# Scaling of the second norm on ScalarE instead of VectorE, in an attention and mixture-of-experts kernel

## The chip, the cores and the metric

The kernel runs on one core of one Trainium2 chip. The time is the device time of one execution in microseconds. An execution is one launch; several runs were made, and their median is the kernel's time. TensorE (PE, with its weight loads PEld), VectorE (DVE), ScalarE (ACT), GpSimd (POOL) and SyncE (SP) each work through their own list of instructions in order and meet through semaphores.

## The reference

The inputs are 4 sequences of 512 tokens with 256 features and, for each, a context of 64 tokens.

```python
x = x + xattn(layernorm(x), ctx, ctx, Wq, bq, Wk, bk, Wv, bv, We, be)   # 16 heads of 16
x = x + ffn(layernorm(x), router_w, router_b, expert_up, expert_down)

def ffn(x):                                  # 8 experts, 1024 hidden, the best 2 per token
    probs = softmax(x @ router_w + router_b)
    top_w, top_idx = top_k(probs, 2)
    for e in range(8):
        h = gelu(x @ expert_up[e].T)
        output += comb[:, e:e+1] * (h @ expert_down[e].T)
```

The layer norm has no learned scale: `(x - mean) / sqrt(var + 1e-5)`. The change is in the second one, ahead of the router.

## The kernel before

The work has two stages. The first takes the four sequences (batches) in turn: norm, attention, residual, second norm, router, and the place of each token in its expert's list. The second walks over tiles of 128 rows gathered by expert. Each engine's program is written by hand, in the order in which it is to run, and a loop step `batch(i)` works on two or three batches at once: it ends batch i−1 (attention output, second norm, logits), begins batch i (queries, scores, exponentials) and, from i = 2 on, does the routing of batch i−2. There are three such steps (i = 1, 2, 3), called steps 1, 2 and 3 here, and then a tail that ends the last batch alone.

A batch is four tiles of 128 tokens (`LT` = 4). Around the second norm this happens:

- VectorE, `residual_norm2` (line 766): for each half (two tiles) it adds the attention's output to `xall` (771), takes statistics (776, 781) and writes `var2` (783). GpSimd makes `rstd2` from it by a power of −0.5 (`halves_rstd2`, 347, line 345). After both halves VectorE scales all four tiles into `xr` (789), by mean and rstd per row. Then come the routing's one-hots of batch i−2, `puts` (872, lines 877 and 879), eight pairs in a ring of four buffers, so the fifth pair waits until TensorE has used the first; and then `logits` (795), whose first instruction is `lg` (798).
- TensorE: `project_out`, `max_turn` (turned maxima, 1165), `scores_turned` of pairs 0 to 3 (1171; pair 3 waits for the first exponential, whose bank it takes), `x2_turn` (turns `xr` into features by tokens, 1240), `slots` (1282), `logits` (1249), `logits_turn` (1255), `slots` again. The next step begins with `values` (1195, 1196), which waits for `lg`.
- ScalarE: `max_turn` (copies the turned maxima, 494), `exps` 0 to 3 (503), `x2_turn` (copies the turned tiles to `x2T`, 525), `logit_copy` (530), `router_exp` (534).
- SyncE: `store` writes `xall` to `out` and `xr`, with the routing weights in its last 8 columns, to `rows` (315). The second stage gathers from `rows`. Before the weights of experts 2 to 7 overwrite `xall`, SyncE waits for the stores of `xall` (325).

The semaphore `v_xn2` counts the scaled tiles; only TensorE's `x2_turn` waits for it (1237).

Of the kernel before, what the change touches and what calls it, by code (L numbers as in the profile page):

```python
# [102 lines left out]
def build(nc, x, ctx_t, ctx_t2, wq, wk, wv, we, bqk, bv, be, router_w, router_b, up, down, const, out, rows):  # L103
    with ExitStack() as ctx:
# [6 lines left out]
        def sem(name):  # L111
            return ctx.enter_context(nc.semaphore(name))
# [4 lines left out]
        def c(name):  # L117
# [44 lines left out]
        mv2 = sb("mv2", [P, LT, 2])  # L162
        var2 = sb("var2", [P, LT])
        rstd2 = sb("rstd2", [P, LT])
        xr = sb("xr", [P, LT, XROW])
        x2T = sb("x2T", [P, LT, KD, P])
        lg, lgs, ex, pr = (sb(n, [P, LT, NE]) for n in ("lg", "lgs", "ex", "pr"))
# [75 lines left out]
            sem(n) for n in "v_wsplit v_k v_stat1 v_var1 v_xn v_xT v_q v_max".split())  # L243
        v_nmh, v_nml, v_rden, v_rdh, v_rdl, v_att, v_at, v_x1 = (
            sem(n) for n in "v_nmh v_nml v_rden v_rdh v_rdl v_att v_at v_x1".split())
        v_stat2, v_var2, v_xn2, v_lg, v_pr, v_top, v_mk, v_msum = (
            sem(n) for n in "v_stat2 v_var2 v_xn2 v_lg v_pr v_top v_mk v_msum".split())
        v_seen, v_comb, v_mbf, v_mtot, v_pos, v_key, v_hot, v_put = (
            sem(n) for n in "v_seen v_comb v_mbf v_mtot v_pos v_key v_hot v_put".split())
        v_pack, v_tab, v_slot, v_done, v_fxT, v_gate, v_fhT, v_y = (  # L250
# [17 lines left out]
        @block.sync  # L268
        def _(sp):
            x_t = x.rearrange("(t p) d -> p t d", p=P)  # L270
            sp.dma_start(xall[:, 0:LT, :], x_t[:, 0:LT, :]).then_inc(d_x0, 16)
            sp.dma_start(cst[:, 0:EARLY], const[:, 0:EARLY]).then_inc(d_const, 16)

            def rows_of(a):
                return a.rearrange("(k p) n -> p k n", p=P)

            def raw_w(n):
                return wraw[:, n, :].rearrange("p (k n) -> p k n", k=KD)


            sp.dma_start(raw_w(1), rows_of(wk)).then_inc(d_k, 16)
            sp.dma_start(ctxT[:, :, :], rows_of(ctx_t)).then_inc(d_k, 16)
            sp.dma_start(bias[:, :, :], bqk.rearrange("p (j k) -> p j k", k=KD)).then_inc(d_k, 16)
            sp.dma_start(raw_w(0), rows_of(wq)).then_inc(d_q, 16)
            sp.dma_start(xall[:, LT:NTOK, :], x_t[:, LT:NTOK, :]).then_inc(d_x, 16)
            sp.dma_start(raw_w(2), rows_of(wv)).then_inc(d_v, 16)
            sp.dma_start(ctxT2[:, :, :, :].rearrange("p k b s -> p k (b s)"), rows_of(ctx_t2)).then_inc(d_v, 16)
            sp.dma_start(raw_w(3), rows_of(we)).then_inc(d_we, 16)
            sp.dma_start(cst[:, EARLY:NCONST], const[:, EARLY:NCONST]).then_inc(d_sel, 16)
            sp.wait_ge(g_rw, 1)  # L290
            sp.dma_start(rw[:, :, 0:NE], rows_of(router_w)).then_inc(d_w, 16)
            sp.dma_start(bv_b[:, :], bv.rearrange("(a n) -> a n", a=1).broadcast_to([P, D])).then_inc(d_w, 16)
            sp.dma_start(be_b[:, :], be.rearrange("(a n) -> a n", a=1).broadcast_to([64, D])).then_inc(d_w, 16)
            sp.dma_start(rb[:, :], router_b.rearrange("(a n) -> a n", a=1).broadcast_to([P, NE])).then_inc(d_w, 16)

            sp.wait_ge(g_zero, 2)
            zeros = zero_r[:, :].bitcast(F32)
            zeros_d = zeros.rearrange("p (a n) -> p a n", a=1).broadcast_to([P, KD, P])
            sp.dma_start(rows[T:T + P, 0:D].rearrange("p (a n) -> p a n", a=KD), zeros_d).then_inc(d_zero, 16)
            sp.dma_start(rows[T:T + P, D:XROW], zeros[:, 0:NE]).then_inc(d_zero, 16)  # L300
            sp.dma_start(out[T:T + P, :].rearrange("p (a n) -> p a n", a=KD), zeros_d).then_inc(d_zero, 16)


            def load01(i):
                if not (isinstance(i, int) and i == 0):
                    sp.wait_ge(v_w01, 2 * i)
                sp.dma_start(raw01[:, 0, :], up[bass.ds(i, 1)].rearrange("a p n -> (a p) n")).then_inc(d_raw01, 16)
                sp.dma_start(raw01[:, 1, :], down[bass.ds(i, 1)].rearrange("a p n -> (a p) n")).then_inc(d_raw01, 16)

            def store(g):  # L310
                sp.wait_ge(v_x1, 2 * g + 2)
                sp.dma_start(out[bass.ds(g * L, L), :].rearrange("(t p) d -> p t d", p=P),
                             xall[:, bass.ds(g * LT, LT), :]).then_inc(d_x1, 16)
                sp.wait_ge(v_comb, g + 1)
                sp.dma_start(rows[bass.ds(g * L, L), :].rearrange("(t p) d -> p t d", p=P),
                             xr[:, :, :]).then_inc(d_rows, 16)

            load01(0)
            with sp.Fori(1, B) as i:
                load01(i)  # L320
                store(i - 1)
            store(B - 1)


            sp.wait_ge(d_x1, 16 * B)
            for e in range(2, NE):
                for q in range(8):
                    if e > 2 and q % 2 == 0:
                        sp.wait_ge(v_wlo, 8 + 4 * (e - 3) + q // 2 + 1)
                    src = (up if q < 4 else down)[2 * e + q // 2 % 2]  # L330
                    sp.dma_start(raw[:, q * 512:(q + 1) * 512], src[:, (q % 2) * 512:(q % 2 + 1) * 512])\
                        .then_inc(d_rawu if q < 4 else d_rawd, 16)
# [119 lines left out]
        def _(act):  # L452
# [64 lines left out]
            def att_high(b):  # L517
                for k in range(KD):
                    act.wait_ge(v_att, KD * b + k + 1)
                    a.activation(at_h[:, k, :], av[:, k, :], ACT.Identity).then_inc(a_at, 1)  # L520

            def x2_turn(b):
                for n in range(2):
                    act.wait_ge(p_x2T, 2 * b + n + 1)
                    a.activation(x2T[:, 2 * n:2 * n + 2, :, :].rearrange("p t k l -> p (t k l)"), bankA[:, n, :], ACT.Identity)\
                        .then_inc(a_x2T, 1)
# [38 lines left out]
            def batch(i):  # L565
                av_copy(i - 1, 0)
                x_high(i, 0)
                exps(i - 1, range(4, 8))
                x_high(i, 1)
                den_copy(i - 1)  # L570
                av_copy(i - 1, 1)
                q_high(i)
                rden_turn(i - 1)
                att_high(i - 1)
                high01(i)
                max_turn(i)
                exps(i, range(4))
                x2_turn(i - 1)
                logit_copy(i - 1)
                router_exp(i - 1)  # L580
# [6 lines left out]
            av_copy(B - 1, 1)  # L587
            rden_turn(B - 1)
            att_high(B - 1)
            x2_turn(B - 1)  # L590
            logit_copy(B - 1)
            router_exp(B - 1)
# [70 lines left out]
        def _(dve):  # L663
# [102 lines left out]
            def residual_norm2(b):  # L766

                for n in range(2):
                    dve.wait_ge(p_proj, 2 * b + n + 1)
                    xs = xall[:, bass.ds(b * LT + 2 * n, 2), :]  # L770
                    v.tensor_tensor(xs, bankB[n][:, :].rearrange("p (t d) -> p t d", t=2), xs, ALU.add)\
                        .then_inc(v_x1, 1)
                    dve.wait_ge(v_x1, 2 * b + n + 1)
                    settle(5)
                    for k in (2 * n, 2 * n + 1):
                        v.bn_stats(stat2[:, k, :], xall[:, bass.ds(b * LT + k, 1), :]
                                   .rearrange("p a d -> p (a d)")).then_inc(v_stat2, 1)
                    dve.wait_ge(v_stat2, 8 * b + 4 * n + 2)
                    settle(6)
                    for k in (2 * n, 2 * n + 1):  # L780
                        v.bn_aggr(mv2[:, k, :], stat2[:, k, :]).then_inc(v_stat2, 1)
                    dve.wait_ge(v_stat2, 8 * b + 4 * n + 4)
                    v.tensor_scalar(var2[:, 2 * n:2 * n + 2], mv2[:, 2 * n:2 * n + 2, 1], EPS, None, ALU.add)\  # L783
                        .then_inc(v_var2, 1)
                if not (isinstance(b, int) and b == 0):
                    dve.wait_ge(d_rows, 16 * b)
                for k in range(LT):
                    dve.wait_ge(g_rstd2, 2 * b + k // 2 + 1)
                    v.tensor_scalar(xr[:, k, 0:D], xall[:, bass.ds(b * LT + k, 1), :].rearrange("p a d -> p (a d)"),
                                    mv2[:, k, 0:1], rstd2[:, k:k + 1], ALU.subtract, ALU.mult).then_inc(v_xn2, 1)  # L790

            def bc3(ap, n):
                return ap.rearrange("p (q a) -> p q a", a=1).broadcast_to([P, ap.shape[1], n])
# [306 lines left out]
        def _(pe):  # L1100
# [133 lines left out]
            def x2_turn(b):  # L1234
                for n in range(2):
                    for t in range(2):
                        pe.wait_ge(v_xn2, LT * b + 2 * n + t + 1)
                        for k in range(KD):
                            o = (t * KD + k) * P
                            last = nc.tensor.transpose(bankA[:, n, o:o + P], xr[:, 2 * n + t, k * P:(k + 1) * P], ident)  # L1240
                    last.then_inc(p_x2T, 1)
# [223 lines left out]
```

## Time and profile before

| | |
|---|---|
| median of 3 runs | 467.22 us (465.77 to 470.2) |
| the profiled execution | 466.3 us, of it 464.5 us span |
| first stage | until about 192 us, the rest is the second stage |
| busy: PE, DVE, ACT, POOL | 85%, 53%, 42%, 36% of the span |
| mean granted TensorE clock | 0.934 of full |

The span runs from the first instruction to the last. A group's busy time says how long an engine worked, not that anything waited for it; the chain of waits says what ended last, and the order in time says what an engine did between. "Granted clock" is the share of TensorE's full clock that the throttle let through: 1.00 is 2.4 GHz, 0.50 is 1.2 GHz. The times at the start of a row are microseconds from the start of the span.

### The profile page before, as it was taken

The numbers are of one execution on the slowest core, as the hardware profiler recorded it, in microseconds if no ns is written. First come the engines' busy times: TensorE is split into PE (matmuls) and PEld (weight loads), VectorE is DVE, ScalarE is ACT, GpSimd is POOL, SyncE is SP. The second block draws the span as 40 slices with busy tenths as digits, with TensorE's granted clock in tenths as the row PEclk, the third lists the DMA queues.
The fourth block names the chain that finished last, engine by engine and source line by source line (L and its number), as shares of the span: only waits on it lengthen the run. The fifth ranks groups of instructions, "written<-read, shape, count | busy, mean of one in ns | idle before, by whom it ended". The sixth has DMA issues, their size and how long they took to land.

```text
span 464.5 us, 9448 instructions
## 1 busy us (share of the span) xinstructions
PE 396.3 (85%) x2154; PEld 315.9 (68%) x2155; DVE 244.7 (53%) x693; ACT 194.2 (42%) x356; POOL 166.0 (36%) x266
## 2 busy tenths in 40 slices
PE   3799897889988674499999899989898999999970
PEld 2575675666666452278888787878787888888860
DVE  3394768887789455723336437364554355333230
ACT  1265433333434312034437346556473464354430
POOL 2315022020301000224454554554546536545541
PEclk9799999998999955589999999999999999999995
DMA  8702010410401101711223627262736222222221
GB/s 277 279 2 90 1 47 0 139 45 1 137 0 54 39 0 48 244 29 24 49 34 93 168 34 215 46 204 48 211 81 173 42 36 46 34 38 42 46 34 11
DMA packets 24784, 36.49 MB, mean 79 GB/s; under 512 B 3136, under 2 KB 15872, under 8 KB 24768
## 3 DMA queue, kind: packets, MB, share of 16 engines
q1 hardware_dynamic: 17760, 26.44, 16.8%
q0 software_dynamic: 7008, 9.86, 13.4%
q8 instruction: 7, 0.11, 0.1%
q14 instruction: 9, 0.07, 0.0%
HBM read 27.04 MB, written 9.24 MB: 78 GB/s over the span
## 4 chain that ended last, share of the span: by engine, by line
PE 56%; issue 16%; DMA 7%; DVE 7%; POOL 5%; ACT 4%; POOLq 1%; ACTq 1%; SPq 0%; DVEq 0%
PE bankC L1385 10%; PE bankC L1106 7%; PE bankC L1108 7%; PE bankC L1107 7%; DMA xr<-rows,idx_g 5%; PE bankC L1386 5%; PE bankB L1363 5%; PE bankA L1355 2%; PE bankB L1106 2%; POOL idx_g L408 2%; PE bankA L1195 1%; PE bankM L1282 1%; POOL rstd L345 1%; PE bankB L1108 1%; PE bankB L1107 1%
## 5 line engine op out<-in xcount | busy, mean ns | idle before, releaser
L1385 PE MATMUL bankC<-dn_w,q_h 128*128 x288 | 104.7, 403 | 1.2 <-DVE q_l L1041 1.2
L1386 PE MATMUL bankC<-dn_w,q_l 128*128 x288 | 80.6, 280 | 0.0
L425 POOL DMA_INDIRECT out<-x2T,idx_s x36 | 58.0, 1612 | 21.3 <-issue 21.3
L1385 PEld LDWEIGHTS bankC<-dn_w,q_h 128*128 128x128 f32 x288 | 54.1, 188 | 12.4 <-issue 1.4
L1106 PE MATMUL bankC<-up_w,xnT_h 128*128 (+1 forms) x144 | 61.0, 424 | 0.9 <-DVE xnT_l L1035 0.9
L1048 DVE SCALAR_TENSOR_TENSOR x2T<-bankC,gate,x2T 128x256 f32<-128x256 f32 x36 | 17.4, 483 | 81.7 <-ACT x2T L614 63.2
L1108 PE MATMUL bankC<-up_w,xnT_l 128*128 (+1 forms) x144 | 57.9, 402 | 0.0
L1107 PE MATMUL bankC<-up_w,xnT_h 128*128 (+1 forms) x144 | 57.5, 399 | 0.0
L1386 PEld LDWEIGHTS bankC<-dn_w,q_l 128*128 128x128 f32 x288 | 54.2, 188 | 0.0
L609 ACT ACTIVATE raw<-bankC 128x512 f32<-128x512 f32 x72 | 43.1, 599 | 24.6 <-PE bankC L1108 24.6
L414 POOL DMA_INDIRECT xr<-rows,idx_g x38 | 42.6, 1120 | 22.3 <-issue 21.7
L1041 DVE TENSOR_TENSOR q_l<-bankB,q_h 128x512 fp32r<-128x512 f32 x72 | 46.1, 681 | 0.8 <-ACT q_h L605 0.7
L345 POOL TENSOR_TENSOR rstd<-var,cst 128x2 f32<-128x2 f32 (+2 forms) x10 | 9.4, 938 | 94.5 <-DVE var L783 87.3
L614 ACT ACTIVATE x2T<-bankC,gate 128x256 f32<-128x256 f32 x36 | 17.0, 472 | 60.6 <-PE bankC L1386 58.6
L389 POOL TENSOR_TENSOR prime<-prime 1x1 f32<-1x1 f32 x74 | 13.7, 185 | 76.4 <-DVE x2T L1048 64.6
L605 ACT ACTIVATE q_h<-bankB 128x512 fp32r<-128x512 f32 x72 | 38.9, 595 | 0.3 <-PE bankB L1363 0.3
L1363 PE MATMUL bankB<-cst,raw 128*128 128x128 f32 x288 | 37.5, 273 | 0.5 <-ACT raw L609 0.5
L600 ACT ACTIVATE xnT_h<-bankA 128x256 fp32r<-128x256 f32 x37 | 14.3, 388 | 53.1 <-PE bankA L1355 51.9
L1363 PEld LDWEIGHTS bankB<-cst,raw 128*128 128x128 f32 x288 | 32.8, 141 | 2.2 <-ACT raw L609 0.8
L408 POOL COPY idx_g<-slot 128x1 int32 (+1 forms) x38 | 28.7, 754 | 15.6 <-DVE slot L972 14.9
L1035 DVE TENSOR_TENSOR xnT_l<-bankA,xnT_h 128x256 fp32r<-128x256 f32 x37 | 15.6, 423 | 32.5 <-ACT xnT_h L600 32.5
L1108 PEld LDWEIGHTS bankC<-up_w,xnT_l 128*128 128x128 f32 x144 | 27.6, 192 | 6.7
(215 smaller groups left out, 726.9 us busy)
## 6 DMA issues: line engine op xcount, KB each, us to landing
xall<-up SPq DMA_DIRECT2D x24, 256.0 KB
xall<-down SPq DMA_DIRECT2D x24, 256.0 KB
rows<-xr SPq DMA_DIRECT2D x4, 528.0 KB, 3.3
raw<-up SPq DMA_DIRECT2D x4, 512.0 KB, 4.5
raw<-down SPq DMA_DIRECT2D x4, 512.0 KB, 5.4
out<-xall SPq DMA_DIRECT2D x4, 512.0 KB, 2.8
xall<-x SPq DMA_DIRECT2D x1, 1536.0 KB, 8.5
cst<-const SPq DMA_DIRECT2D x1, 640.0 KB, 8.4
```

The source lines that it names most:

```text
L408: g.tensor_copy(idx_g[:, ring:ring + 1], slot[:, bass.ds(col, 1)]).then_inc(g_gi, 1)
L414: g.indirect_dma_start(xr[:, ring, :], None, rows, bass.IndirectOffsetOnAxis(idx_g[:, ring:ring + 1], 0), bounds_check=T + P - 1).then_inc ...
L425: g.indirect_dma_start(out, bass.IndirectOffsetOnAxis(idx_s[:, 0:1], 0), y, None, bounds_check=T + P - 1, compute_op=ALU.add).then_inc(d_a ...
L605: a.activation(hT_h[:, n * 512:(n + 1) * 512], bankB[n][:, :], ACT.Identity).then_inc(a_fhT, 1)
L609: a.activation(hbuf[:, n * 512:(n + 1) * 512], bankC[:, n, :], ACT.Gelu).then_inc(a_gelu, 1)
L1041: v.tensor_tensor(hT_l[:, o], bankB[n][:, :], hT_h[:, o].bitcast(F32), ALU.subtract)\
L1106: mm(out_, left_h, right_h, start=first, stop=False)
L1107: mm(out_, left_h, right_l, start=False, stop=False)
L1108: return mm(out_, left_l, right_h, start=False, stop=last)
L1363: last = nc.tensor.transpose(bankB[n][:, m * P:(m + 1) * P], hbuf[:, o:o + P], ident)
L1385: mm(bankC[:, 2, :], hT_h[:, o], wd, start=(m == 0), stop=False)
L1386: last = mm(bankC[:, 2, 0:D], hT_l[:, o], wd[:, 0:D], start=False, stop=(m == KF - 1))
```

## The change

VectorE no longer scales the tiles. For each half it computes `nmr2` = −mean · rstd, two columns. ScalarE does the scaling as `Identity(scale · x + bias)` with `scale` = `rstd2` and `bias` = `nmr2`, a column each, for the two tiles of a half. In a loop step the first half's two activations stand between ScalarE's `max_turn` and the first exponential, the second half's between the second and the third exponential; in the tail both stand ahead of `x2_turn`. The semaphore that counts the scaled tiles is now ScalarE's. SyncE waits for the last scaling before it loads over `xall`, since ScalarE now reads `xall` last.

```diff
+        nmr2 = sb("nmr2", [P, LT])
...
             sp.wait_ge(d_x1, 16 * B)
+            sp.wait_ge(a_xn2, LT * B)
...
+            def norm2(b, n):
+                act.wait_ge(v_nmr, 2 * b + n + 1)
+                for k in (2 * n, 2 * n + 1):
+                    a.activation(xr[:, k, 0:D], xall[:, bass.ds(b * LT + k, 1), :].rearrange("p a d -> p (a d)"),
+                                 ACT.Identity, bias=nmr2[:, k:k + 1], scale=rstd2[:, k:k + 1]).then_inc(a_xn2, 1)
...
                 max_turn(i)
-                exps(i, range(4))
+                norm2(i - 1, 0)
+                exps(i, range(2))
+                norm2(i - 1, 1)
+                exps(i, range(2, 4))
                 x2_turn(i - 1)
...
             att_high(B - 1)
+            norm2(B - 1, 0)
+            norm2(B - 1, 1)
             x2_turn(B - 1)
...
-                for k in range(LT):
-                    dve.wait_ge(g_rstd2, 2 * b + k // 2 + 1)
-                    v.tensor_scalar(xr[:, k, 0:D], xall[:, bass.ds(b * LT + k, 1), :].rearrange("p a d -> p (a d)"),
-                                    mv2[:, k, 0:1], rstd2[:, k:k + 1], ALU.subtract, ALU.mult).then_inc(v_xn2, 1)
+                for n in range(2):
+                    dve.wait_ge(g_rstd2, 2 * b + n + 1)
+                    v.scalar_tensor_tensor(out=nmr2[:, 2 * n:2 * n + 2], in0=mv2[:, 2 * n:2 * n + 2, 0], scalar=-1.0,
+                                           in1=rstd2[:, 2 * n:2 * n + 2], op0=ALU.mult, op1=ALU.mult).then_inc(v_nmr, 1)
...
-                        pe.wait_ge(v_xn2, LT * b + 2 * n + t + 1)
+                        pe.wait_ge(a_xn2, LT * b + 2 * n + t + 1)
```

## Rows read from the trace of the kernel before

**Rows 1.** The page's first part: busy us, share of the span, instructions.

```profile
PE 396.3 (85%) x2154; PEld 315.9 (68%) x2155; DVE 244.7 (53%) x693; ACT 194.2 (42%) x356; POOL 166.0 (36%) x266
```

**Rows 2.** The chain of waits, end of step 1: start us, us, what ran.

```profile
69.14 1.05 PE bankB L1249 x16
...
71.26 1.39 PE bankA L1195 x8
72.65 0.86 PE bankB L1196 x8
```

**Rows 3.** ACT in order of time: start us, us, line, tiles [idle before, releaser].

```profile
68.41 1.08 ACT L525 ACTIVATE x2T<-bankA 128x512 f32<-128x512 f32 x2
...
100.69 0.60 ACT L494 ACTIVATE nmxT<-bankC 128x512 fp32r<-128x512 f32 x1 [5.37 <-PE bankC L1168]
102.66 0.60 ACT L503 ACTIVATE prob<-bankC 128x512 f32<-128x512 f32 x1 [1.37 <-PE bankC L1183]
...
105.36 0.60 ACT L503 ACTIVATE prob<-bankC 128x512 f32<-128x512 f32 x1 [0.32 <-PE bankC L1183]
105.85 1.08 ACT L525 ACTIVATE x2T<-bankA 128x512 f32<-128x512 f32 x2
...
143.37 1.08 ACT L525 ACTIVATE x2T<-bankA 128x512 f32<-128x512 f32 x2
```

**Rows 4.** DVE in order of time, steps 1, 2 and 3.

```profile
64.69 0.73 DVE L789 TENSOR_SCALAR xr<-xall,mv,rstd 128x256 f32<-128x256 f32 x2
...
102.37 2.32 DVE L789 TENSOR_SCALAR xr<-xall,mv,rstd 128x256 f32 x4
...
106.42 0.27 DVE L877 TENSOR_SCALAR hot<-cst,lrow 128x128 fp32r<-128x128 f32 x1
...
108.36 0.19 DVE L798 TENSOR_TENSOR lg<-bankB,rb 128x32 f32<-128x32 f32 x1
...
139.91 2.31 DVE L789 TENSOR_SCALAR xr<-xall,mv,rstd 128x256 f32 x4
```

**Rows 5.** POOL in order of time, step 2: the second half's rstd.

```profile
102.44 0.70 POOL L345 TENSOR_TENSOR rstd<-var,cst 128x2 f32<-128x2 f32 x1 [1.75 <-DVE var L783]
```

**Rows 6.** PE in order of time, step 2.

```profile
104.23 0.40 PE L1106 MATMUL bankC<-q_h,kbd_h 128*128 128x512 f32 x1
...
105.16 1.04 PE L1240 MATMUL bankA<-cst,xr 128*128 128x128 f32 x8
```

**Rows 7.** All engines in order of time, the tail.

```profile
175.88 0.73 DVE L789 TENSOR_SCALAR xr<-xall,mv,rstd 128x256 f32<-128x256 f32 x2
176.05 0.80 POOL L345 TENSOR_TENSOR rstd<-var,cst 128x2 f32<-128x2 f32 x1 [3.47 <-DVE var L783]
...
176.88 0.73 DVE L789 TENSOR_SCALAR xr<-xall,mv,rstd 128x256 f32<-128x256 f32 x2 [0.27 <-POOL rstd L345]
...
178.50 0.60 ACT L525 ACTIVATE x2T<-bankA 128x512 f32<-128x512 f32 x1 [0.40 <-PE bankA L1240]
```

**Rows 8.** Lines by form, the whole span: min/median/max ns, first and last start.

```profile
L600 ACT ACTIVATE xnT_h<-bankA x37: 384/385/417, 196.9 to 443.8; 128x256 fp32r<-128x256 f32 x37
...
L614 ACT ACTIVATE x2T<-bankC,gate x36: 452/474/477, 210.4 to 451.8; 128x256 f32<-128x256 f32 x36
...
L525 ACT ACTIVATE x2T<-bankA x8: 589/598/604, 68.4 to 178.5; 128x512 f32<-128x512 f32 x8
...
L520 ACT ACTIVATE at_h<-av x8: 630/632/633, 54.8 to 164.1; 128x512 fp32r<-128x512 f32 x8
...
L861 DVE SCALAR_TENSOR_TENSOR lrow<-ltile,rank x4: 166/166/582, 83.7 to 186.1; 128x8 f32<-128x8 f32 x4
```

**Rows 9.** The chain, then a stretch with engines' busy us and PE's clock.

```profile
109.73 2.26 PE bankA L1195 x8
111.99 1.56 PE bankB L1196 x8
...
111.00:112.00 1.00, 1.00 (x10) 0.69 (x5) 1.00 (x2) 0.00 (x0) 0.00 (x0) 0.50 0.00 0
```

More of the change, by code:

```diff
@@ L245, in build @@
             sem(n) for n in "v_nmh v_nml v_rden v_rdh v_rdl v_att v_at v_x1".split())
-        v_stat2, v_var2, v_xn2, v_lg, v_pr, v_top, v_mk, v_msum = (
-            sem(n) for n in "v_stat2 v_var2 v_xn2 v_lg v_pr v_top v_mk v_msum".split())
+        v_stat2, v_var2, v_nmr, a_xn2, v_lg, v_pr, v_top, v_mk, v_msum = (
+            sem(n) for n in "v_stat2 v_var2 v_nmr a_xn2 v_lg v_pr v_top v_mk v_msum".split())
         v_seen, v_comb, v_mbf, v_mtot, v_pos, v_key, v_hot, v_put = (
```

## The prediction

> **What bounds the kernel now.** I read the busy shares first, then the chain of waits, then the order in time of ACT, DVE, POOL and PE around the second norm. The shares say that TensorE carries the kernel (85%), with VectorE at 53% and ScalarE at 42% [rows 1]; an average tells nothing of one stage, so it only says that a microsecond taken off VectorE is worth nothing unless VectorE is late somewhere. The chain shows where: between the turned scores of one batch and the values product of the next, the time runs copy of x2T, logits, copy of lgT, turn of the logits, `lg`, and only then the values; the logits and the values product of step 1 stand in it [rows 2]. This is a relay with nothing beside it on TensorE but a few small products. So the question is when the second x2T copy ends, in each of the four batches.
>
> The exponentials of the same stage sit ahead of these copies in ScalarE's queue [rows 3]. In batch step 2 ScalarE turns the maxima at 100.69, runs the four exponentials from 102.66 to 105.96, paced by TensorE's turned scores, and ends the two copies at 105.85 + 1.08 = 106.93. VectorE scales the four tiles from 102.37 to 104.69 [rows 4]; TensorE wants them only at 105.16 [rows 6]. The scaling has half a microsecond of slack there, and ScalarE has only the gaps between its exponentials, about 0.3 each: 105.36 + 0.60 − 102.66 = 3.30 for four exponentials that need about 2.1 back to back.
>
> **The change part by part.** *Removed from VectorE:* four tensor-scalars per batch, 2.32 in step 2 and 2.31 in step 3 [rows 4]. *Added on VectorE:* two products of 128x2 per batch. The nearest row is the scalar-tensor-tensor of 128x8, 0.166 [rows 8]. The first is queued behind both halves' statistics, as the scaling was, so it starts where the scaling starts now (102.37). The second waits for the second rstd (102.44 + 0.70 = 103.14 [rows 5]), which the first two scalings cover today. VectorE is free for the routing's one-hots at about 103.4 instead of 102.37 + 2.32 = 104.7.
>
> *What that is worth.* The first four one-hot pairs come 1.2 earlier. The fifth can't: it waits for TensorE's first slot product, which stands behind the x2 turn (105.16 + 1.04 = 106.20 [rows 6]), and it runs today at 106.42, hard on that [rows 4]. So the last one-hot moves by a tenth or two, and `lg` (108.36, no idle before it) today begins as both VectorE and the turned logits are ready. I take the relief at nothing: it moves off a path that TensorE closes at the same moment.
>
> *Added on ScalarE:* four activations of 128x256 per batch, from SBUF, with scale and bias each a column. No row has this form, so I bound it. Without an operand from a column the 128x256 copy takes 0.385, with one 0.474 (the difference 0.089), and a 128x512 copy takes 0.632 from SBUF against 0.598 from PSUM, so 0.034 more [rows 8]. With two columns that makes 0.385 + 0.178 + 0.034 = 0.60. The lower end is 0.474, the one-column row; the upper 0.69, by doubling the step for each column. Two copies of 0.598 end 1.08 after the first starts [rows 3], so neighbours overlap by 0.11, and one costs the queue 0.50 (0.37 to 0.59). Less than the lower end is excluded, since no form of this size costs under it with a column. I take 0.50, as every part of it has a row. The Trainium skill (ScalarE: Activation LUTs, "What ACT_TABLE_LOAD costs") gives 186 ns + 0.833 ns per element and about 93 ns for each [128,1] operand, so 0.585 here; by it the queue's price would be 0.49 and the sum some 0.2 less. Its step for one column agrees with the 0.089; no run here yet shows the second.
>
> *Moved and waited for.* ScalarE now waits, behind the turned maxima, for the first product, then does two scalings, two exponentials, two scalings, two exponentials, two copies. From the first scaling on nothing is left to wait for: the scores are there, the second product too. Eight pieces at 0.50 and the copies' 1.1 make 5.1. A releaser's end and the start of what it frees lie 0.03 to 0.05 apart (rstd ends 176.05 + 0.80 = 176.85, the scaling starts 176.88 [rows 7]).
>
> - Step 2: 102.37 + 0.17 + 0.05 = 102.59; plus 5.1 is 107.69, against 106.93: **+0.76**.
> - Step 3: 139.91 + 0.22 + 5.1 = 145.23, against 143.37 + 1.08 = 144.45 [rows 3, 4]: **+0.78**.
> - Step 1: 64.69 + 0.22 + 5.1 = 70.01, against 68.41 + 1.08 = 69.49: **+0.52**.
>
> What is queued behind: the first exponential ends at 102.59 + 1.00 + 0.60 = 104.19, and TensorE's fourth turned scores, which need its bank, start at 104.23 today [rows 6], so TensorE is just not held. The scaled tiles three and four arrive at 105.2 and 105.7; TensorE turns them from 105.16 on at 0.13 each, so it loses a tenth at most. The later exponentials feed a product of the next step, microseconds off. The copies are what is late, and everything behind them moves by as much; neither `lg` nor the values have slack to take it back.
>
> - The tail (last batch), where nothing lies beside it: today the scalings start at 175.88 and 176.88, and the second copy ends at 178.50 + 0.60 = 179.10 [rows 7]. After: first product until 176.05, scalings from 176.10 to 177.20; second product 176.88 to 177.05, scalings 177.1 to 178.2 instead of 177.61. The copy starts 178.50 − 177.61 = 0.89 after the last scaling today, a little of it TensorE's backlog. That gives **+0.55**.
>
> The wait added to SyncE before the expert loads costs nothing: ahead of it stands the store of the last batch's rows, which needs the routing weights, and these come after the scalings. If that cover went, SyncE would load at 178.2, still earlier than now. POOL has the same work in the same order; it only starts each batch's key blocks as much later as TensorE's scores end.
>
> Sum: 0.52 + 0.76 + 0.78 + 0.55 = **2.6**. With 0.37 for a piece each loop step is 0.5 less and the tail 0.3: 0.8 in all. With 0.59 each is 0.36 more: 4.0. Against the profiled execution that is 466.3 + 2.6 = 468.9. The median of the three runs, 467.22, stands 0.9 above it, and the forecast goes by the median, as the times of the rivals below do: 467.2 + 2.6 = 469.8.
>
> **Rivals.**
> 1. *TensorE's clock falls once or twice more.* The values product of the step after 2 runs at the lower level of 1.2 GHz: the granted clock is 0.50 of full at 111 to 112, after a stretch in which TensorE waited in short pieces for copy, turn and slots. It takes 2.26 + 1.56 = 3.82 [rows 9] where step 1's takes 1.39 + 0.86 = 2.25 at full speed [rows 2]: 1.57 for a fall. Step 1 and 3 have similar short idles and no fall today, and the change lengthens exactly these idles by 0.5 to 0.8. One more fall gives 469.8 + 1.6 = 471.4; both give 473.0, which is 5.8 or 1.2% slower than before. This is the rival on the other side: it decides from the second additional fall on. For it: nothing but the idle sets the three places apart. Against: step 1 has about as much idle as step 2 and did not fall. 15% for one, 10% for both or a longer low stretch.
> 2. *The fall goes away.* Moved by under a microsecond, the same product may find the clock high: 469.8 − 1.6 = 468.2. 10%. The Trainium skill (TensorE: Matmul & The Clock Gate, Part 1) says that the activity monitor runs freely and isn't started by the kernel, so the place of a change varies from run to run; by that rule rivals 1 and 2 both occur in some executions of either kernel. One trace can't show it; the three runs' spread of 4.4 doesn't speak against it.
> 3. *VectorE's relief counts.* If `lg` is held by the one-hots and not by the turned logits, each routed step gains up to 1.2, and ScalarE's scalings would hide in its gaps: 467.2 − 2.4 = 464.8. For it: `lg` starts with no idle before it [rows 4]. Against: the fifth one-hot waits for TensorE, and ScalarE's gaps between the exponentials (3.30 − 2.1 = 1.2 in all) don't hold four scalings (2.0). 7%.
> 4. *A third of the loss.* TensorE or VectorE takes some of the delay back, or a scaling is as cheap as the one-column copy: 467.2 + 0.8 = 468.0. 13%.
>
> **How the numbers follow.** The forecast has 45%, rival 1 25%, rival 2 10%, rival 3 7%, rival 4 13%. About 1% (4.7) is what can be told from no change. Inside it lie all cases but the double fall (10%) and the high price with one fall, 4.0 + 1.6 = 5.6 (4%): slower 0.14. Faster needs rival 3 together with a lost fall, 2.4 + 1.6 = 4.0, and some spread beside it: 0.03. Within 1%: 0.83. The range goes down to rival 4's price with the fall gone, 467.2 + 0.8 − 1.6 = 466.4, and up to the high price with one more fall, 467.2 + 4.0 + 1.6 = 472.8; outside it lie rival 3 and the worst of rival 1.
>
> **What would show it.** In the changed trace: a scaling of 0.55 to 0.65 on ScalarE; the first one 0.2 after the first-half product's start; the four exponentials no longer idle before them; the x2T copies' end 0.5 to 0.8 later after the maxima's turn than 106.93 − 100.69 = 6.24; `lg` with idle before it in steps 2 and 3 where it has none. Wrong if the copies end no later (scaling cheaper or started before both halves' statistics are done), if `lg` doesn't follow them, or if the count of low-clock stretches differs from today's, which would shift the time by 1.6 for each.

## The result

The changed kernel takes 471.42 us (median of 22 runs, 467.15 to 475.44), the kernel before 467.65 (22 runs, 464.22 to 470.36). The ratio is 1.0071, with 95% interval 1.0048 to 1.0095: 3.3 us slower, between 2.2 and 4.4. The ratio leaves out five of the changed kernel's executions as slow (474.25 to 475.44), so it is under the 3.8 by which the two medians differ. The forecast was 469.8 in a range of 466.4 to 472.8, and 2.6 of it the change's own.

The profiled execution of the changed kernel has a span of 468.8 against 464.5. Its first part of the page shows what was moved, VectorE 4 us less busy and ScalarE 7 more, against [rows 1]:

```profile
PE 400.6 (85%) x2154; PEld 317.3 (68%) x2155; DVE 240.8 (51%) x685; ACT 201.0 (43%) x372; POOL 165.4 (35%) x266
```

ScalarE in order of time, steps 1, 2 and 3, where [rows 3] have the same stage before:

```profile
62.77 0.60 ACT L496 ACTIVATE nmxT<-bankC 128x512 fp32r<-128x512 f32 x1 [5.28 <-PE bankC L1181]
...
68.40 1.09 ACT L533 ACTIVATE x2T<-bankA 128x512 f32<-128x512 f32 x2
...
100.71 0.60 ACT L496 ACTIVATE nmxT<-bankC 128x512 fp32r<-128x512 f32 x1 [5.37 <-PE bankC L1181]
102.69 1.09 ACT L527 ACTIVATE xr<-xall,nmr,rstd 128x256 f32 x2 [1.38 <-DVE nmr L802]
103.69 1.06 ACT L505 ACTIVATE prob<-bankC 128x512 f32<-128x512 f32 x2
104.64 1.08 ACT L527 ACTIVATE xr<-xall,nmr,rstd 128x256 f32 x2
105.63 1.07 ACT L505 ACTIVATE prob<-bankC 128x512 f32<-128x512 f32 x2
106.58 1.09 ACT L533 ACTIVATE x2T<-bankA 128x512 f32<-128x512 f32 x2
...
137.33 0.60 ACT L496 ACTIVATE nmxT<-bankC 128x512 fp32r<-128x512 f32 x1 [5.30 <-PE bankC L1181]
...
143.21 1.09 ACT L533 ACTIVATE x2T<-bankA 128x512 f32<-128x512 f32 x2
```

From 102.69 on no row has an idle bracket: scalings, exponentials and copies run back to back, where the exponentials before had 0.25 to 0.33 of idle between them. The stage from the start of the maxima's copy to the end of the second x2T copy takes 69.49 − 62.77 = 6.72, 107.67 − 100.71 = 6.96 and 144.30 − 137.33 = 6.97. Before it took 6.24, 6.24 and 6.22. That is +0.48, +0.72 and +0.75.

VectorE in order of time, step 2, against [rows 4]:

```profile
102.39 0.16 DVE L802 SCALAR_TENSOR_TENSOR nmr<-mv,rstd 128x2 f32<-128x2 f32 x1
103.19 0.69 DVE L802 SCALAR_TENSOR_TENSOR nmr<-mv,rstd 128x2 f32<-128x2 f32 x1 [0.64 <-POOL rstd L347]
103.80 0.28 DVE L890 TENSOR_SCALAR hot<-cst,lrow 128x128 fp32r<-128x128 f32 x1
...
106.50 0.29 DVE L890 TENSOR_SCALAR hot<-cst,lrow 128x128 fp32r<-128x128 f32 x1 [0.50 <-PE bankM L1295]
...
109.10 0.19 DVE L811 TENSOR_TENSOR lg<-bankB,rb 128x32 f32<-128x32 f32 x1 [0.70 <-PE bankB L1268]
```

The relief is there and buys nothing: VectorE waits 0.50 for TensorE's first slot product ahead of the fifth one-hot, and 0.70 for the turned logits ahead of `lg`, which had no idle before it. In both kernels `lg` starts 1.43 after the second x2T copy ends (108.36 − 106.93 and 109.10 − 107.67).

The tail, ScalarE in order of time, against [rows 7]; the second half's statistics end on VectorE at 178.15:

```profile
178.26 2.08 ACT L527 ACTIVATE xr<-xall,nmr,rstd 128x256 f32<-128x256 f32 x4 [11.38 <-DVE nmr L802]
180.25 0.57 ACT L533 ACTIVATE x2T<-bankA 128x512 f32<-128x512 f32 x1
181.12 0.60 ACT L533 ACTIVATE x2T<-bankA 128x512 f32<-128x512 f32 x1 [0.30 <-PE bankA L1253]
```

**Where the span's 4.3 us are.** Both traces, divided at the same events:

| stretch | before | after | difference |
|---|---|---|---|
| start to maxima's copy of step 1 | 63.25 | 62.77 | −0.48 |
| to that of step 2 | 37.44 | 37.94 | +0.50 |
| to that of step 3 | 37.54 | 36.62 | −0.92 |
| to the start of the last `var2` (DVE) | 37.57 | 40.65 | +3.08 |
| to the first gather (POOL) | 17.12 | 17.56 | +0.44 |
| second stage | 271.58 | 273.26 | +1.68 |

Part of these differences is not the path (the chain of waits that sets the time) but TensorE's clock. A *fall* is here a stretch of 4 to 5 us in which the granted clock is at its lower level. In the rows below stand the stretch, its length, the busy us of PE, PEld, DVE, ACT and POOL with their instructions, the granted clock (third from the end), and the DMA share and GB/s; the first row is of the kernel before, the others of the changed one:

```profile
109.00:115.00 6.00, 5.57 (x27) 3.20 (x27) 3.85 (x7) 1.36 (x3) 0.00 (x0) 0.72 0.01 3
```

```profile
109.00:115.00 6.00, 5.52 (x34) 4.06 (x34) 5.09 (x12) 2.01 (x4) 0.00 (x0) 1.00 0.00 0
146.00:151.00 5.00, 4.85 (x27) 1.92 (x27) 3.20 (x26) 0.83 (x2) 0.00 (x0) 0.66 0.11 37
157.00:161.00 4.00, 3.14 (x17) 0.60 (x10) 0.00 (x0) 0.77 (x2) 0.00 (x0) 0.57 0.00 0
338.00:342.00 4.00, 4.00 (x17) 3.43 (x16) 0.42 (x1) 0.56 (x2) 1.65 (x4) 0.57 0.42 67
```

The fall behind step 2 is gone. Two others came behind step 3, and one in the second stage, where the change does nothing.

### The profile page after: what moved, and what is told of

Its sections match the earlier page's. It is cut to its first block, busy times and chain, and to the rows that moved or that the text cites. A ratio compares the mean times of both kernels' runs of the same rounds, so it can differ in the third digit from the quotient of the medians.

```text
span 468.8 us, 9469 instructions
## 1 busy us (share of the span) xinstructions
PE 400.6 (85%) x2154; PEld 317.3 (68%) x2155; DVE 240.8 (51%) x685; ACT 201.0 (43%) x372; POOL 165.4 (35%) x266
## 4 chain that ended last, share of the span: by engine, by line
PE 61%; DVE 9%; issue 9%; DMA 7%; ACT 6%; POOL 3%; POOLq 1%; ACTq 1%; DVEq 1%; SPq 0%
PE bankC L1398 10%; PE bankC L1119 7%; PE bankC L1121 7%; PE bankC L1120 7%; DMA xr<-rows,idx_g 5%; PE bankC L1399 5%; PE bankB L1376 5%; PE bankB L1119 3%; PE bankB L1121 2%; PE bankB L1120 2%; PE bankA L1368 2%; POOL idx_g L410 2%; PE bankA L1208 2%; PE bankB L1209 1%; PE bankB L1241 1%
## 5 line engine op out<-in xcount | busy, mean ns | idle before, releaser
L1398 PE MATMUL bankC<-dn_w,q_h 128*128 x288 | 107.4, 411 | 1.2 <-DVE q_l L1054 1.2
L1399 PE MATMUL bankC<-dn_w,q_l 128*128 x288 | 81.7, 284 | 0.0
L1119 PEld LDWEIGHTS bankC<-up_w,xnT_h 128*128 128x128 f32 x144 | 27.7, 192 | 6.3 <-DVE xnT_l L1048 1.3
```

The costliest lines, as they stand in the source:

```text
L1119: mm(out_, left_h, right_h, start=first, stop=False)
L1398: mm(bankC[:, 2, :], hT_h[:, o], wd, start=(m == 0), stop=False)
L1399: last = mm(bankC[:, 2, 0:D], hT_l[:, o], wd[:, 0:D], start=False, stop=(m == KF - 1))
```

## The experiments

The ratios are to runs of the kernel before on the same chip. "Stage" is the one from the start of the maxima's copy to the end of the second x2T copy in steps 1, 2, 3. "Low" counts the stretches of lower clock in the profiled execution, leaving out the one near 14 to 22 at the start, the tail's (from about 160 to 205, in all kernels without filler) and the last ten us, in which TensorE has run out of work.

The experiments are read by the time from event to event, which the last part of e5 puts side by side.

**e1: the loop as changed, the tail back on VectorE.**

```diff
+                if b == B - 1:      # the four tensor-scalars of before
...
-            norm2(B - 1, 0)
-            norm2(B - 1, 1)
```

> The loop steps as changed, the tail's four scalings back on VectorE. Theory A (ScalarE's queue ahead of the x2T copies carries the loss): from the start of the copy of the turned maxima to the end of the second x2T copy 6.7 to 7.0 us in each of the steps 1 to 3 (6.24 before, 6.72, 6.96 and 6.97 in the changed kernel); tail as before, 3.2 us from VectorE's first scaling to the end of the second copy; time 1.9 us over the kernel before. Rival B (the loss is TensorE clock that happens to fall): the same stage lengths, but the time differs from before by more or less than 1.9 by multiples of about 1.5, by the count of low stretches in the trace.

Measured: 472.13 (4 runs), ratio 1.0147 (1.0099 to 1.0195). Stage 6.71, 6.96, 6.96; from the last `var2` to the first gather 17.13, as before (17.12) and 0.43 less than with the change. So both parts of theory A hold in the trace, and the time doesn't follow: the ratio gives 6.9 us over before where A said 1.9, and the median is above the full change's. That is what rival B described. Its trace has four low stretches, at 81, 111, 149 and 159, three more than before's, and three at 1.5 with A's 1.9 make 6.4; its first gather comes 5.9 later than before's, counted from step 1's maxima copy. A single execution's span says nothing of a path difference of half a microsecond.

**e2: the first product early.**

```diff
                         .then_inc(v_x1, 1)
+                    if n == 1:
+                        product(b, 0)          # nmr2 of the first half, waits for its rstd
...
+                product(b, 1)
```

> The first half's product is computed right after VectorE has added the second half's residual, instead of after both halves' statistics; all else as changed. Theory A': part of the loss is that ScalarE stands idle for 1.4 us between the turned maxima and the first scaling. Then the first two scalings run in that gap, the four exponentials start within 0.1 us of where they did before, and the stage from maxima copy to second x2T copy takes 6.3 to 6.5 us instead of 6.96. Tail: first two scalings before 175, the second two as changed, 0.4 us over before. Time 0.7 to 1.0 us over before. Rival C (the placement between the exponentials delays TensorE's scores through the banks): stage stays at 6.8 or more.

Measured: 467.75, ratio 1.0028 (1.0005 to 1.0052). ScalarE in order of time, step 2:

```profile
100.83 0.60 ACT L496 ACTIVATE nmxT<-bankC 128x512 fp32r<-128x512 f32 x1 [5.37 <-PE bankC L1185]
101.42 1.09 ACT L527 ACTIVATE xr<-xall,nmr,rstd 128x256 f32 x2
102.79 0.60 ACT L505 ACTIVATE prob<-bankC 128x512 f32<-128x512 f32 x1 [0.28 <-PE bankC L1200]
...
104.13 1.09 ACT L527 ACTIVATE xr<-xall,nmr,rstd 128x256 f32 x2
...
106.09 1.08 ACT L533 ACTIVATE x2T<-bankA 128x512 f32<-128x512 f32 x2
```

The first two scalings fill the gap, and the first exponential waits for TensorE again. Stage 6.32, 6.34, 6.33: all but 0.1 of the loop's loss is gone. The rival of the banks is out, since the second pair still stands between the exponentials. The tail's stretch is 17.48, 0.36 over before, where 0.4 was expected. Up to the first gather this trace is 0.66 longer than before's, with its low stretch in the first stage in the same place (110); by the ratio the time is 1.3 over (0.2 to 2.4), with a second low stretch at 263. Expected were 0.7 to 1.0.

**e3: no scale and bias.** The scalings become plain copies, so `xr` holds the residual without its norm.

```diff
-                                 ACT.Identity, bias=nmr2[:, k:k + 1], scale=rstd2[:, k:k + 1]).then_inc(a_xn2, 1)
+                                 ACT.Identity).then_inc(a_xn2, 1)
```

> The four activations copy the tile without scale and bias, so that the norm is left out of xr and the routing may differ a little; it prices the two column operands. Price by A: 0.42 us for one activation instead of 0.59, 0.31 instead of 0.50 of queue; stage 6.2 to 6.3 us in steps 2 and 3, that is the whole loop loss is gone; the tail 0.3 us shorter than as changed. Rival D (an activation costs what it moves, operands are free): 0.57 or more for one, stage stays 6.9. The first stage is what is compared, as the second depends on the routing.

Measured: the copy takes 0.414 where the scaling takes 0.592 (median, line 527 of each), so two column operands cost 0.178. Stage 6.21, 6.23, 6.25, as in the kernel before. The whole loop loss hangs on these two operands. The tail's stretch is 17.22, 0.34 less than as changed. Ratio 1.0004 (0.9981 to 1.0028), no low stretch.

**e4: six scalings per batch.**

```diff
                 act.wait_ge(v_nmr, 2 * b + n + 1)
+                if n == 0:
+                    for k in range(2):
+                        a.activation(spill[:, k, :], xall[...], ACT.Identity, bias=nmr2[...], scale=rstd2[...])
```

> ScalarE scales the first half's two tiles twice, once into a buffer nobody reads: two more activations of the same form per batch. By A each adds its 0.50 us to the path in full, in every step and in the tail: stage 7.9 to 8.0 us in steps 2 and 3 (7.7 in step 1), four times 1.0 us in all, time 4 us over the changed kernel and 6.4 over before (1.4%). By rival E (the relay has slack that takes a part back): the stage grows by under 0.6 us for the pair, the time by under 2.5 over the changed kernel.

Measured: 471.47 (4 runs), ratio 1.0097 (1.0065 to 1.0128). ScalarE, step 2:

```profile
103.98 1.09 ACT L529 ACTIVATE spill<-xall,nmr,rstd 128x256 f32 x2 [1.38 <-DVE nmr L807]
104.97 1.08 ACT L532 ACTIVATE xr<-xall,nmr,rstd 128x256 f32 x2
```

The pair costs 104.97 − 103.98 = 0.99. Stage 7.69, 7.93, 7.93, which is 0.96 to 0.97 over the changed kernel; the tail's stretch grows from 17.56 to 18.54. Every stage pays in full, as A said. The time from one step to the next doesn't in every step: step 1 takes 0.97 more than as changed, but step 2 takes only 0.67 more than e1's (38.86 against 38.19, both with a fall at 111). So the relay takes about a third back in a routed step, which is a part of what rival E said; its bounds, under 0.6 for the stage, are missed. This trace and before's have the same low stretches up to the first gather, one behind step 2 and the tail's, so they can be compared directly: the first gather comes 5.6 later (135.26 against 129.67 from step 1's maxima copy), where A said 6.4 for the whole. By the ratios the kernel lies 4.5 us over before (3.0 to 6.0), and 1.2 over the changed kernel (3.3) where A said 4; but the changed kernel's trace has three low stretches to this one's one.

**e5: the first half on ScalarE, early; the second on VectorE.**

```diff
+                        product(b, 0)          # after the second half's residual
...
+                for k in (2, 3):               # VectorE, as before
+                    v.tensor_scalar(xr[:, k, 0:D], ...)
...
-                exps(i, range(2))
-                norm2(i - 1, 1)
-                exps(i, range(2, 4))
+                exps(i, range(4))
```

> Only the first half's two tiles are scaled by ScalarE, from the early product, in its gap behind the turned maxima; the second half's two by VectorE as before. By A the stage from maxima copy to second x2T copy is as in the kernel before, 6.2 to 6.3 us in all steps, since nothing is added ahead of the copies but what fills an idle gap; the tail at most 0.1 us shorter than before's. Time within 0.3 us of before, apart from the number of clock falls. Rival F (VectorE's relief is worth something by itself): 1 us or more faster than before, as the one-hots start 1.1 us earlier.

Measured: 467.58, ratio 1.0020 (0.9991 to 1.0050); stage 6.24, 6.21, 6.22; tail 17.02, 0.10 under before. As A said, and F is out: by the ratio the time is 0.9 over before (−0.4 to 2.3). What it showed beside is worth more: its profiled execution is long (span 469.9), with a path no longer than before's. Stretches as above:

```profile
109.00:113.00 4.00, 3.42 (x17) 1.58 (x16) 3.34 (x6) 0.23 (x1) 0.00 (x0) 0.57 0.01 4
146.00:151.00 5.00, 4.89 (x28) 2.01 (x28) 3.29 (x27) 0.83 (x2) 0.00 (x0) 0.66 0.11 37
157.00:161.00 4.00, 3.13 (x19) 0.78 (x12) 0.00 (x0) 0.98 (x2) 0.00 (x0) 0.57 0.00 0
338.00:342.00 4.00, 4.00 (x16) 3.43 (x15) 0.45 (x2) 0.87 (x2) 2.18 (x5) 0.58 0.41 62
```

These are the places of the changed kernel's falls and of before's together.

The traces of before, the change and e1 to e5, from maxima copy to maxima copy, from step 3's to the last `var2`, and from there to the first gather, with where a fall lies in the interval:

| kernel | step 1 to 2 | step 2 to 3 | step 3 to `var2` | tail |
|---|---|---|---|---|
| before | 37.44 | 37.54 (109) | 37.57 | 17.12 |
| changed | 37.94 | 36.62 | 40.65 (147, 157) | 17.56 |
| e1 | 39.36 (81) | 38.19 (111) | 40.88 (149, 159) | 17.13 |
| e2 | 37.55 | 37.68 (110) | 37.62 | 17.48 |
| e3 | 37.44 | 36.11 | 37.55 | 17.22 |
| e4 | 38.91 | 38.86 (111) | 38.95 | 18.54 |
| e5 | 37.38 | 37.34 (109) | 39.67 (146, 157) | 17.02 |

Equal paths with and without a fall give its price: 39.36 − 37.94 = 1.42 in step 1, 37.54 − 36.11 = 1.43 and 38.19 − 36.62 = 1.57 in step 2.

**e6, e7, e8: filler on TensorE**, under the kernel before, the changed one and e5's.

```diff
+            def fill(n, bank):
+                for _ in range(n):
+                    mm(bank, wq_h[:, 0, 0:P], wq_h[...], start=True, stop=True)   # 128x512, result unread
...
+                fill(2, bankB1[:, :])
                 logits(i - 1)
+                fill(1, bankB1[:, :])
                 logits_turn(i - 1)
...
+                fill(1, bankB1[:, :])
...
+            fill(9, spare)                     # 3, 4, 2, 9, 8, 1, 12, 8 at the tail's waits
             project_out(B - 1)
```

> The kernel before, with matmuls of 128x512 on constant data into a bank nobody reads, put into TensorE's waits: 2 ahead of the logits, 1 ahead of their turn and 1 behind it in each loop step, 3 to 12 at the waits of the tail and of the second stage's start. Clock theory (short waits let the granted clock fall, and each low stretch costs about 1.5 us, the tail's from 161 to 202 about 6): the granted clock stays at 1.00 from 100 to 200, the tail's output projection takes 4.6 us instead of 8.2, the first up-product 2.9 instead of 5.2, and the time is 5 to 8 us under before. Rival G (the filler sits on the path): each wait ends up to 0.3 us later and the clock stays as it was, time 1 to 3 us over before.

> The changed kernel with the same filler matmuls. With the clock held high in the first stage, what is left between this and the kernel before with filler is the path alone. Theory A: 2.2 to 2.6 us slower than that one (0.5, 0.7, 0.75 in the steps and 0.45 in the tail; 0.0 to 0.3 of it may be hidden, as the filler makes the first one late there but not here), with the same low stretches in both. Rival B (the measured 3.3 us are in good part clock): with the clocks alike the distance falls from 3.3 to about 2.4; if it stays at 3.3 or more, B is out and something else is on the path.

> The kernel with the first half on ScalarE and the second on VectorE, with the same filler. By A it stands within 0.3 us of the kernel before with filler. By F it is 1 us or more faster than that.

Measured: 461.21, 462.54 and 462.34 (6, 6 and 7 runs); ratios 0.9929 (0.9883 to 0.9974), 0.9934 (0.9892 to 0.9976), 0.9907 (0.9862 to 0.9952). The granted clock of the kernel before from 100 to 190, and then of e6 from 100 to 180 and from 185 to 190:

```profile
100.00:190.00 90.00, 69.59 (x383) 48.28 (x383) 65.89 (x255) 28.24 (x50) 11.03 (x14) 0.82 0.17 55
```

```profile
100.00:180.00 80.00, 71.87 (x428) 50.42 (x428) 61.28 (x233) 28.28 (x50) 11.05 (x14) 1.00 0.14 47
185.00:190.00 5.00, 4.85 (x16) 3.58 (x15) 3.35 (x27) 0.00 (x0) 2.23 (x6) 0.66 0.81 283
```

The clock stays up through the tail, except from 185 to 190, where the filler itself then runs long. By the ratios e6 gains 3.3 us (1.2 to 5.5), by the medians 4.9; expected were 5 to 8, and the filler that runs long is a part of what is missing. Rival G has only that place. Between e6 and e7, whose low stretches in the first stage are nearly in the same places (80 and 185, 81 and 187), the first gather is at 187.44 and 189.46; counted from step 1's maxima copy (62.08 and 62.44) it is 1.66 later. For this distance A said 2.2 to 2.6; the medians are 1.3 apart and the ratios 0.2, so neither A nor B has its number. Between e6 and e8 the times settle nothing (e8 is 1.1 slower by the medians and 1.0 faster by the ratios, where A said within 0.3 and F 1 or more faster), but the traces do: from step 2's maxima copy to step 3's they take 36.35 and 36.30, so VectorE's relief is worth nothing there.

**e9 to e12: filler placed better**, under before, the change, e5's and e1's.

```diff
+                    fill(between, bankC[:, 2, :])   # 1 behind each of the last batch's slot products
...
-            fill(12, spare)
+            fill(14, spare)                    # ahead of the counts; 9 instead of 12 ahead of the table's turn
```

> The kernel before with the filler matmuls placed better in the tail: one behind each of the eight slot products, 14 instead of 12 ahead of the counts, 9 instead of 12 ahead of the table's turn. In the first filler version the clock was at the lower level from 185 to 190 and the filler ahead of the table's turn took 4.56 us there and ran 0.8 us past the work it waited for. Clock theory: no low stretch between 100 and 200, time 0.5 to 1.5 us under the first filler version, 6 us under before. Rival G (more filler only gets in the way): time as the first version's or over it.

> The changed kernel with this filler. Theory A: 1.7 to 2.4 us slower than the kernel before with it, from trace to trace at the first gather 2.0 us later (measured with the first filler: 189.46 against 187.44), as the path is longer and the clock the same. Rival B' (with the clock held up the two are alike): under 1 us apart.

> First half on ScalarE from the early product, second half on VectorE, with this filler. Theory A: within 0.5 us of the kernel before with this filler; rival F (VectorE's relief is worth something): 1 us or more under it.

> The loop steps as changed, the tail's scaling on VectorE, with this filler. Without filler this kernel came out slower than the full change, though it has less of it: 472.1 against 471.4 us, with four low stretches between 80 and 165 in its trace. Theory A with clock by chance: with the clock held up it lies 0.4 to 0.5 us under the full change with filler and 1.4 to 1.9 over before with filler. Rival H (the tail's scaling is really better on ScalarE): at or over the full change with filler.

| kernel with filler | median | ratio to before | low |
|---|---|---|---|
| e9, before | 461.92 | 0.9874 (0.9830 to 0.9917) | 81, 156, 194 |
| e10, changed | 462.89 | 0.9898 (0.9869 to 0.9927) | 80, 175, 192 |
| e12, loop changed | 461.66 | 0.9883 (0.9840 to 0.9925) | 81 |
| e11, first half early on ScalarE | 460.11 | 0.9866 (0.9815 to 0.9917) | 81 |

Filler doesn't rule falls out (no low stretch between 100 and 200 was expected, e9 has two), and whether the second placement is better than the first (0.9874 against 0.9929 for the kernel before) the intervals leave open. The order of the four medians is nearly that of their paths, but the intervals overlap by far; e10 and e9 lie 1.0 apart, where A said 1.7 to 2.4. A part of the reason is in the filler itself: two of the matmuls stand ahead of the logits, so they make the kernel before late where the changed one waits anyway. In step 2 of e9 the second x2T copy ends at 108.11, but the two run until 108.63, and the logits start at 108.56; in e10 the weights of the last twelve logit products load at 108.59, as the copy ends (108.54). From step 2's maxima copy to step 3's e9 takes 138.32 − 101.87 = 36.45 and e10 138.32 − 101.58 = 36.74, 0.29 apart instead of the 0.51 of the traces without filler. So this pair doesn't give the path's price by its time. e12 against e10 (1.2 less by the medians, 0.4 to 0.5 expected) has the sign that A said, inside the intervals; rival H, that ScalarE is the better place in the tail, has nothing for it, as the tail's stretch is 0.43 longer there in the traces without filler, and 17.37 in e10 against 16.15 in e12 (a fall at 175 is in e10's). e11 against e9 is 1.8 less by the medians, which is rival F's sign, and 0.4 by the ratios. The traces are against F: the two take 38.88 and 38.86 from step 1 to 2, 36.58 and 36.45 from step 2 to 3, and differ in step 3, where e9 has its fall at 156 (35.93 against 34.22).

The best version is e11's: 460.11 us, 1.3% under before, and as fast as e9 within the interval. Nearly all of it comes from the filler, not from where the norm is scaled.

## Why the prediction was right, point by point

- *Price of a scaling*: 0.60 forecast, 0.592 measured; of its place in the queue 0.50, measured 0.99 for a pair. The build-up from an operand's step (0.089, twice) and SBUF's 0.034 holds: e3 has 0.178 for the two operands, and the plain copy from SBUF 0.414 against 0.385 from PSUM. The Trainium skill (ScalarE: Activation LUTs, "What ACT_TABLE_LOAD costs") has 186 ns + 0.833 ns per element and about 93 ns for each column operand, which gives 0.585 as an estimate for this form; the trace agrees within 0.01.
- *The stage*: +0.52, +0.76, +0.78 forecast; +0.48, +0.72, +0.75 measured. e3 and e4 show that it is ScalarE's queue: 0.18 less for a scaling takes it all away, two more scalings add 0.97.
- *The tail*: +0.55 forecast, +0.44 measured from the last `var2` to the first gather; e1 takes back 0.43. The part of the 0.89 that was TensorE's backlog was larger than I allowed.
- *"Everything behind them moves by as much"*: so in step 1 (37.94 − 37.44 = 0.50 for 0.48) and in the tail. In step 2 a part doesn't arrive. Its interval to step 3 without a fall is 36.62 as changed and 36.11 in e3, whose stage is before's: 0.51 of 0.72. Of the 0.21, 0.07 are ahead of the values product (it starts 2.76 after the second copy's end in e3, 2.69 as changed) and the rest behind it, for which I have no cause. For step 3 there is no such pair. e4 has 1.38 over before for 1.71 of stage, and four fifths of the changed kernel's 0.75 would be 0.60; against e5, with falls in nearly the same places, the changed kernel is 0.98 longer.
- *VectorE's relief*, put at nothing: `lg` keeps its 1.43 behind the copy, and the values product gains at most the 0.1 by which 2.69 is under before's 2.80. That VectorE would be free at about 103.4 was a little early: the second product took 0.69 and not 0.17, and the first one-hot ran at 103.80. As TensorE closes this path, it cost nothing.
- *Sum*: 2.6 forecast. By the traces 0.50 + 0.51 + 0.44 and 0.60 to 0.98 for step 3, 2.1 to 2.4. The ratio's interval (2.2 to 4.4) and this meet at its lower end only, so something else is in the measured 3.3.
- *Rival 1* (one or two more falls) happened in the profiled execution, two in the first stage and one in the second, and *rival 2* (the fall behind step 2 goes away) in the same one. The forecast's own sign of being wrong, another count of low stretches than before's, came with it. Its price for a fall, 1.6, holds (1.42 to 1.57). I had treated the two rivals as alternatives, as if each kernel had its number of falls. The traces of e1 to e5 have 4, 2, 0, 1 and 4 low stretches, with no relation to the path: most in e1 and in e5, whose path is before's, one in e4, whose path is the longest. The Trainium skill's rule (TensorE: Matmul & The Clock Gate, Part 1), that the monitor runs freely and the place of a change varies from run to run, fits this. No kernel was profiled in a second execution here, so the variation within one kernel is seen only in its times, which spread by 6 us before and 8 after, and in the mean granted clock of each execution, which goes from 0.924 to 0.948 in the 55 executions of the kernel before that the experiments are compared with.
- *Rival 3* is out by e5 (1.0020, interval 0.9991 to 1.0050). *Rival 4* is out, as the price was the forecast's.

**Where the other 1 us is.** The mean granted clocks point to it. In the 22 executions of the changed kernel they go from 0.920 to 0.937, with a mean of 0.929; the mean of the 55 of the kernel before is 0.935. At a lower level of half the clock, 0.006 of 469 us is some 6 us more at that level in each execution, more than one fall of 4 to 5 us. This is an estimate, and a rough one: the mean also counts the last ten us, where the clock is low and nothing waits, and the 55 were not taken side by side with the 22. Side by side are e1, with the same loop steps, at 0.927 to 0.932, and its 19 of the kernel before at 0.931 to 0.941. At the 1.42 to 1.57 that a fall costs it is enough for the 1 us between 2.1 to 2.4 by the path and 3.3. So the changed kernel seems to have been longer at the lower clock on average, and rival 1 has come true in part. That the total lies within 1 us of the forecast's 2.6 is owed to both: a path somewhat shorter than forecast and a clock that the forecast had left to a rival.

Why it would fall more often stays open. Longer waits on TensorE (0.70 instead of none ahead of `lg`) would be a reason, but e4 speaks against it: it has the longest waits, and three of its four executions have 0.939, above before's mean. That fits its ratio, 4.5 us where its path alone gives 5.6; but there are only these four.

## What to carry to other kernels

Before moving work to a less busy engine, look at what stands behind the new place in that engine's own queue. ScalarE was idle more than half of the time, and yet each 0.5 us put ahead of a copy that the next engine waited for made that copy 0.5 late, while with the first pair 1.3 to 1.4 us earlier, in the queue's own gap, the four of them cost the stage 0.1 in place of 0.7. Then look on to the next stage: of 0.7 in a routed step 0.5 arrived. Where TensorE's clock falls by chance, compare stage by stage between the same events: e1 and e4 came out in the wrong order by their times (1.0147 and 1.0097, with intervals that overlap), and in the right one by every stage. And read the mean granted clock of every execution beside its time; it told of falls that one trace can't count.

## What the runs showed of the hardware

An activation of 128x256 from SBUF takes 0.414 plain and 0.592 with scale and bias from columns; neighbours overlap by 0.1. With filler matmuls the granted clock is 1.00 from 100 to 180 in e6 (0.82 on average from 100 to 190 without them). They take 0.7 to 1.3% off the whole (ratios 0.9934 to 0.9866), which is the largest effect of the study, though single falls remain. The output projection of the last batch ran from 165.57 to 173.95 before, and from 164.78 to 169.69 in e6. In the kernel before TensorE was busy 8.38 of the 9 us from 165 to 174, and the granted clock stayed at 0.50 all the while: once low, it did not rise by this work.
